# GNN kernel on one core: first row of equal rows from sums of powers of two on TensorE, and the histogram's high-part numbers read from PSUM

## The chip, the cores and the metric

The kernel runs on 1 core of one Trainium2 chip. The metric is the device time of one execution in microseconds (us), and the median over several executions is compared. The engines are named as in the profile: PE is TensorE (PEld its weight loads), DVE is VectorE, ACT is ScalarE, POOL is GpSimd, SP is SyncE; a q behind a name (PEq, DVEq, POOLq) is the engine's instruction queue.

## The reference, cut to what matters

100,000 nodes with 32 features pass through four graph layers that share one list of 50,000 edges sorted by destination; each layer adds its result to x. The change touches two things that the layers need. The first is a table that says, for each node, where its row of edge results lies (`pos_table`), which takes a histogram of the destinations. The second is the neighbour sum of the third layer, in which both ends of an edge give to each other:

```python
rows = jnp.concatenate([i, j]); cols = jnp.concatenate([j, i])
neighbor_sum = jax.ops.segment_sum(conical[cols], rows, num_segments=N_NODES)   # conical: 16 features
deg = jax.ops.segment_sum(jnp.ones_like(rows, dtype=x.dtype), rows, num_segments=N_NODES)
agg = neighbor_sum / jnp.clip(deg, 1.0)[:, None]
```

The part of this sum that goes to the sources of the edges (unsorted) is the scatter with addition that the stage called symmetric below does.

## The kernel before

Edges are padded to 14 chunks (EC) of 28 x 128 (C = 28 edges on each of P = 128 partitions), nodes to 28 chunks (NC) of 28 x 128. The program is a row of stages, each a block in which the engines run lists of their own and meet only at semaphores; at the end of a block all engines wait for each other, so the next stage starts when the last engine is through. In order: `stage_tables`, `stage_attention`, `stage_sage_first`, `stage_sage_second`, `stage_symmetric`, `stage_third_layer`, `stage_relations`. In most of them POOL issues 392 indirect DMAs (one for each of 14 x 28 columns, 128 rows each) one after another.

`stage_tables` (tiles named a_...). POOL makes the constants (L326 to L340), then issues 392 gathers of x by destination into `x_dst` (L342, L343), and last waits for all of them to land. Beside it DVE and PE make the histogram: a destination is cut into a low part (10 bits) and a high part (98 values, HIGH). For each chunk `hot_high` (L350 to L354) compares the high parts of 28 columns with the numbers 0 to 97 in one DVE `tensor_tensor` (is_equal) of 128 x 2744; both its inputs, `part` (float32) and the first 98 columns of `wide` (float16), lie in SBUF, and its result is float16. `hot_low` (L356 to L362) makes four one-hots of 1024 columns of the low parts with `tensor_scalar`, and PE multiplies them (L498) into the count of each of 98 x 1024 nodes. `hot_high` is called 14 times, `hot_low` 98 times. From the counts come the positions (L440 to L451), which are stored; then DVE, ACT and SP normalise the 28 node chunks and store them (L452 to L461, L474 to L479, L313 to L318). `Norm` holds its means in a PSUM bank of 512 columns of which `Norm.USED` = 112 are in use.

`stage_symmetric` (tiles named e_..., L1315 to L1408). Each chunk holds 28 columns of 128 target positions `posF`. Two rows of a column with the same target may not be added by the same indirect DMA, so they are first summed: PE spreads the positions of a column over the partitions (L1392, into PSUM `pB`), DVE compares them with `posF` (L1371, `eq`, 128 x 3584), and PE multiplies `eq` with the 17 values of each row (L1399, into `pS`), which leaves in each row the sum over all equal rows. Only the first of the equal rows may then be written to its target; the others go to a trash row of their own. DVE finds the first by masking `eq` with the triangle `g.before` (L1373, `tensor_tensor`, both inputs in SBUF), summing over the row (L1376, `rank`) and testing for zero (L1378); the index is stored at L1382 as int32. ACT copies the sums to SBUF (L1408), and POOL issues 28 indirect DMAs that add (L1349 to L1357). Index and value buffers are double; DVE and ACT wait, before they write one again, for the adds of two chunks earlier (`wait_added`). The values themselves are made by `sum_back` (L1411 to L1416, two `tensor_tensor`).

Of the kernel before, what the change touches and what calls it, by code (L numbers as in the profile page):

```python
# [4 lines left out]
f32 = mybir.dt.float32  # L5
f16 = mybir.dt.float16
i32 = mybir.dt.int32
ALU = mybir.AluOpType
ACT = mybir.ActivationFunctionType
AX = mybir.AxisListType  # L10

P = 128
F = 32
N, E = 100000, 50000
C = 28
# [14 lines left out]
HIGH = NPAD // LOW  # L30
HID1, HID2 = 64, 128
CON = 16
CW = CON + 1
# [9 lines left out]
def bc_feat(ap, n=F):  # L43
    return ap.unsqueeze(2).to_broadcast([ap.shape[0], ap.shape[1], n])


def bc_tile(ap, n):
    return ap.unsqueeze(1).to_broadcast([ap.shape[0], n, ap.shape[1]])
# [183 lines left out]
def stage_tables(nc, g):  # L232
# [3 lines left out]
    with ExitStack() as ctx, g.sem.stage():  # L236
        sb = lambda name, shape, dt=f32: ctx.enter_context(nc.sbuf_tensor(f"a_{name}", shape, dt))
        S = lambda name: g.sem(f"a_{name}")
# [4 lines left out]
        part = sb("part", [P, 2, ET])  # L243
        wide_i = sb("wide_i", [P, LOW], i32)
        wide = sb("wide", [P, LOW], f16)
        base_i = sb("base_i", [HIGH, LOW], i32)
        base = sb("base", [HIGH, LOW])
        ones = sb("ones", [HIGH, LOW])
        upto, has = sb("upto", [HIGH, LOW]), sb("has", [HIGH, LOW])
        first = sb("first", [HIGH, 1])  # L250
# [22 lines left out]
        flags, all_done, all_kept, deg_rowed, deg_back = S("flags"), S("all_done"), S("all_kept"), S("deg_rowed"), S("deg_back")  # L273
        block = ctx.enter_context(nc.Block())
        w = g.norm

        @block.sync
        def _(sp):
# [70 lines left out]
        def _(dve):  # L349
            def hot_high(c):  # L350
                if c > 1:
                    dve.wait_ge(hots_used, (c - 1) * (C // GROUP))
                nc.vector.tensor_tensor(hoth[:, c % 2], bc_feat(part[:, 1, c * C:(c + 1) * C], HIGH),
                                        bc_tile(wide[:, 0:HIGH], C), ALU.is_equal)  # L354

            def hot_low(n):  # L356
                if n > 1:
# [43 lines left out]
            dve.drain().then_inc(padded, 1)  # L401
            dve.wait_ge(made, 1)
            nc.vector.tensor_copy(wide[:], wide_i[:])
            nc.vector.tensor_copy(base[:], base_i[:])
            nc.vector.tensor_copy(g.relid[:], g.relid_i[:])
            nc.vector.tensor_copy(g.trash[:], g.trash_i[:])
# [120 lines left out]
def part(c):  # L527
    return slice(c * C, (c + 1) * C)
# [785 lines left out]
def stage_symmetric(nc, g):  # L1314

    with ExitStack() as ctx, g.sem.stage():
        sb = lambda name, shape, dt=f32: ctx.enter_context(nc.sbuf_tensor(f"e_{name}", shape, dt))
        S = lambda name: g.sem(f"e_{name}")  # L1320
        SW = lambda name: g.lasting(f"e_{name}")
        eq, eqb = sb("equal", [P, C, P]), sb("equal_before", [P, C, P])
        val, add = sb("values", [P, 2, C, CW]), sb("add_rows", [P, 2, C, CW])
        aidx = sb("add_idx", [P, 2, C], i32)
        rank, shift = sb("rank", [P, C]), sb("shift", [P, C])
        pB = ctx.enter_context(nc.psum_tensor("e_pB", [P, C * P], f32))
        pS = ctx.enter_context(nc.psum_tensor("e_pS", [P, 512], f32))
        val_ready, spread, eq_ready, summed, add_ready, idx_ready = (
            S(x) for x in ("val_ready", "spread", "eq_ready", "summed", "add_ready", "idx_ready"))
        R = len(g.sums)  # L1330
        added = [SW(f"added{b}") for b in range(R)]
        block = ctx.enter_context(nc.Block())

        def wait_added(eng, c):

            for b in range(R):
                eng.wait_ge(added[b], 16 * len(range(b, (c + 1) * C, R)))

        @block.sync
        def _(sp):  # L1340
            g.sem.clear_before(sp)

        @block.gpsimd
        def _(pool):
            for c in range(EC):
                pool.wait_ge(idx_ready, c + 1)
                pool.wait_ge(add_ready, c + 1)
                for t in range(C):
                    b, turn = (c * C + t) % R, (c * C + t) // R  # L1349
                    if turn:  # L1350
                        pool.wait_ge(added[b], 16 * turn)
                    pool.indirect_dma_start(  # L1352
                        out=g.sums[b], out_offset=bass.IndirectOffsetOnAxis(ap=aidx[:, c % 2, t:t + 1], axis=0),
                        in_=add[:, c % 2, t, :], in_offset=None, bounds_check=NTRASH - 1, oob_is_err=True,
                        compute_op=ALU.add).then_inc(added[b], 16)
            wait_added(pool, EC - 1)

        @block.vector
        def _(dve):
            nc.vector.memset(val[:], 1.0)  # L1360
            dve.drain()
            for c in range(EC):
                a = c % 2
                if c > 1:
                    dve.wait_ge(summed, c - 1)
                sum_back(nc, dve, g, g.con_in[:, c, :], g.con[:, c], c, val[:, a, :, 0:CON])
                dve.drain().then_inc(val_ready, 1)
                dve.wait_ge(spread, c + 1)
                if c:
                    dve.wait_ge(summed, c)  # L1370
                nc.vector.tensor_tensor(eq[:], pB[:].rearrange("p (t k) -> p t k", k=P), bc_feat(g.posF[:, part(c)], P), ALU.is_equal)  # L1371
                dve.drain().then_inc(eq_ready, 1)  # L1372
                nc.vector.tensor_tensor(eqb[:], eq[:], bc_tile(g.before[:], C), ALU.mult)  # L1373
                nc.vector.tensor_scalar(shift[:], g.posF[:, part(c)], g.trash[:, 0:1], None, ALU.subtract)
                dve.drain()
                nc.vector.tensor_reduce(rank[:], eqb[:], AX.X, ALU.add)  # L1376
                dve.drain()
                nc.vector.scalar_tensor_tensor(out=shift[:], in0=rank[:], scalar=0.0, in1=shift[:], op0=ALU.is_equal, op1=ALU.mult)  # L1378
                dve.drain()
                if c > 1:  # L1380
                    wait_added(dve, c - 2)
                nc.vector.tensor_scalar(aidx[:, a, :], shift[:], g.trash[:, 0:1], None, ALU.add)  # L1382
                dve.drain().then_inc(idx_ready, 1)

        @block.tensor
        def _(pe):
            for c in range(EC):
                if c:
                    pe.wait_ge(eq_ready, c)
                for t in range(C):  # L1390
                    n = c * C + t
                    last = nc.tensor.transpose(pB[:, t * P:(t + 1) * P], g.posF[:, n:n + 1].to_broadcast([P, P]), g.ident[:])  # L1392
                last.then_inc(spread, 1)
                pe.wait_ge(eq_ready, c + 1)
                pe.wait_ge(val_ready, c + 1)
                if c:
                    pe.wait_ge(add_ready, c)
                for t in range(C):
                    last = nc.tensor.matmul(pS[:, t * CW:(t + 1) * CW], eq[:, t, :], val[:, c % 2, t, :], start=True, stop=True)  # L1399
                last.then_inc(summed, 1)  # L1400

        @block.scalar
        def _(act):
            for c in range(EC):
                act.wait_ge(summed, c + 1)
                if c > 1:
                    wait_added(act, c - 2)
                nc.scalar.copy(add[:, c % 2].rearrange("p t w -> p (t w)"), pS[:, 0:C * CW]).then_inc(add_ready, 1)  # L1408


def sum_back(nc, dve, g, car, fil, c, out):  # L1411

    K = car.shape[1]
    nc.vector.tensor_tensor(out, bc_tile(car, C), bc_feat(g.suf[:, part(c)], K), ALU.mult)
    dve.drain()
    nc.vector.tensor_tensor(out, out, swap(fil), ALU.add)  # L1416
# [483 lines left out]
def build(nc, A, dbg=()):  # L1900
# [15 lines left out]
    with ExitStack() as ctx:  # L1916
# [16 lines left out]
        with ExitStack() as early:  # L1933
            sb1 = lambda name, shape, dt=f32: early.enter_context(nc.sbuf_tensor(name, shape, dt))
            g.w1l, g.w1r, g.w1gr = sb1("w1l", [P, 2, P]), sb1("w1r", [P, 2, P]), sb1("w1gr", [P, P])
            g.b1col, g.b1out = sb1("b1col", [P, 1]), sb1("b1out", [P, F])
            with ExitStack() as attention:
                sb0 = lambda name, shape, dt=f32: attention.enter_context(nc.sbuf_tensor(name, shape, dt))
                g.w0, g.bias0, g.watt = sb0("w0", [P, P]), sb0("bias0", [P, F]), sb0("watt", [P, 3, F])
                g.precut, g.cut0 = sb0("precut", [P, ET]), sb0("cut_inside", [P, ET])  # L1940
                g.srcI, g.dstI = sb0("src", [P, ET], i32), sb0("dst", [P, ET], i32)
                with g.norm.space():
                    stage_tables(nc, g)
                    stage_attention(nc, g)
            with g.norm.space():
                stage_sage_first(nc, g)
# [57 lines left out]
```

## Time and profile before

| | us |
|---|---|
| median of 3 runs | 4964.66 |
| lowest and highest | 4962.52, 4970.22 |
| the profiled execution, own time | 4980.69 |
| its span, first to last instruction | 4979.0 |
| mean granted TensorE clock | 0.67 |

The profiled execution took 16.0 us more than the median (0.3%); its span is 1.7 us less than its own time. In the profile a number after x counts instructions, a time in square brackets is how long the engine stood idle before the instruction, and the name behind the arrow is what ended that. L12 is line 12 of the kernel. "issue" is time in which an engine waited for nothing that the profile shows. Times in the timeline are us from the start of the span; a row there may merge several instructions (its x says how many).

### The profile page before, as it was taken

How to read it: one execution, taken by the hardware profiler on the slowest of the kernel's cores; microseconds unless marked ns; L12 is line 12 of the kernel's file. 1: busy time of each engine (PE TensorE's matmuls, PEld its weight loads, DVE VectorE, ACT ScalarE, POOL GpSimd, SP SyncE). 2: the span in 40 equal slices, each digit the busy share in tenths (PEclk: the TensorE clock that was granted, in tenths of full speed). 3: DMA queues.
4: the chain of work that ended last, by engine and by line, in shares of the span. 5: the costliest groups of instructions: out<-in, count | busy, mean ns of one | idle time of the engine just before them, and what ended most of it. 6: DMA issues, size and time to landing. Idle time of an engine off the chain costs nothing. (4 is left out here: it accounts for less than half of the span.)

```text
span 4979.0 us, 30430 instructions
## 1 busy us (share of the span) xinstructions
PE 2353.3 (47%) x8870; PEld 1415.7 (28%) x8870; DVE 2972.3 (60%) x3595; ACT 933.8 (19%) x1345; POOL 3530.3 (71%) x3150
## 2 busy tenths in 40 slices
PE   7810156665577760000433222167663756656563
PEld 3400033343344440000433222022221433333332
DVE  8865166665677765566532222066664778778784
ACT  0011011211344431111000000044442111111110
POOL 8877676663777717777488888777774577777774
PEclk9955555555799985555555555588886777777776
DMA  1044243432344432222122222345442011110100
GB/s 27 10 123 134 35 89 88 87 84 68 100 143 144 146 125 64 63 77 64 12 5 5 5 5 5 46 141 156 153 148 63 19 31 27 25 31 21 31 25 11
DMA packets 347736, 327.80 MB, mean 66 GB/s; under 512 B 223248, under 2 KB 295835, under 8 KB 346365
## 3 DMA queue, kind: packets, MB, share of 16 engines
q1 hardware_dynamic: 84368, 236.67, 13.3%
q0 software_dynamic: 144256, 45.62, 10.4%
q10 hardware_dynamic: 118944, 43.56, 3.6%
q8 instruction: 70, 1.15, 0.1%
q14 instruction: 98, 0.79, 0.1%
HBM read 170.38 MB, written 156.58 MB: 66 GB/s over the span
## 5 line engine op out<-in xcount | busy, mean ns | idle before, releaser
L1352 POOL DMA_INDIRECT sum_table<-e_add_rows,e_add_idx x392 | 657.1, 1676 | 173.8 <-issue 118.0
L1704 POOL DMA_INDIRECT out_x<-g_out_rows,end_index x392 | 401.2, 1023 | 224.0 <-issue 122.2
L533 POOL DMA_INDIRECT d_ring<-g_table,pos x392 | 392.9, 1002 | 217.9 <-issue 124.2
L533 POOL DMA_INDIRECT c_ring<-x_table,pos x392 | 396.3, 1011 | 204.1 <-issue 121.9
L533 POOL DMA_INDIRECT g_ring<-x_table,pos x392 | 418.8, 1068 | 172.2 <-issue 119.1
L533 POOL DMA_INDIRECT b_ring<-h_table,src x392 | 404.9, 1033 | 180.0 <-issue 116.0
L343 POOL DMA_INDIRECT x_dst<-in_x,dst x392 | 436.2, 1113 | 133.5 <-issue 133.5
L533 POOL DMA_INDIRECT f_ring<-con_table,pos x392 | 419.3, 1070 | 133.7 <-issue 126.8
L1880 PE MATMUL g_pX<-w,g_h_T 128*128 128x512 f32 x784 | 442.7, 716 | 114.9 <-DVEq L1740 114.8
L1617 PE MATMUL f_pH<-f_T,w2in 128*128 128x448 f32 x672 | 316.8, 617 | 277.8 <-DVE f_T L1509 277.8
L1399 PE MATMUL e_pS<-e_values,e_equal 128*128 128x17 f32 x784 | 168.8, 374 | 418.9 <-DVEq L1372 418.9
L164 ACT ACTIVATE norm_sq<-norm_xc 128x896 f32<-128x896 f32 x168 | 158.1, 949 | 856.2 <-DVE norm_xc L137 683.9
L1382 DVE TENSOR_SCALAR e_add_idx<-e_shift,trash 128x28 int32<-128x28 f32 x14 | 3.5, 248 | 478.7 <-DMA sum_table<-e_add_rows,e_add_idx 478.6
L1399 PEld LDWEIGHTS e_pS<-e_values,e_equal 128*128 128x128 f32 x784 | 167.3, 330 | 422.3 <-DVEq L1372 422.3
L1738 DVE TENSOR_TENSOR g_bases<-g_pX,g_rel 128x1024 f32<-128x1024 f32 x196 | 238.7, 1218 | 44.9 <-PE g_pX L1880 37.5
L1617 PEld LDWEIGHTS f_pH<-f_T,w2in 128*128 128x128 f32 x672 | 135.4, 214 | 450.5 <-DVE f_T L1509 288.7
L1579 ACT ACTIVATE f_hid_T<-f_pH,b2col 128x448 f32<-128x448 f32 x336 | 208.1, 635 | 292.2 <-PE f_pH L1617 275.8
L1880 PEld LDWEIGHTS g_pX<-w,g_h_T 128*128 128x128 f32 x784 | 172.9, 233 | 311.6 <-issue 171.5
L1741 DVE TENSOR_REDUCE g_message<-g_bases 128x64 f32<-128x1024 f32 x196 | 239.4, 1221 | 23.7 <-issue 0.9
L144 DVE TENSOR_REDUCE norm_stat<-norm_sq 128x28 f32<-128x896 f32 x168 | 176.6, 1079 | 90.5 <-ACT norm_sq L164 88.1
L498 PE MATMUL a_pcnt<-a_hot_low,a_hot_high 128*98 128x512 f16 x784 | 198.7, 409 | 46.2 <-DVE a_hot_low L361 45.2
L228 PE MATMUL b_pT<-ident,b_h_node 128*128 128x128 f32 x196 | 49.1, 428 | 314.7 <-DMA b_h_node<-h_table 314.7
(342 smaller groups left out, 5250.4 us busy)
## 6 DMA issues: line engine op xcount, KB each, us to landing
f_sums<-sum_table ACTq DMA_DIRECT2D x126, 238.0 KB
sum_table<-c_zero SPq DMA_DIRECT2D x39, 715.0 KB, 5.3
g_table<-c_g SPq DMA_DIRECT2D x42, 448.0 KB, 2.5
g_etype<-in_etype_rows SPq DMA_DIRECT2D x14, 1204.0 KB
h_table<-a_xp SPq DMA_DIRECT2D x28, 560.0 KB, 3.2
a_x<-in_x SPq DMA_DIRECT2D x28, 448.0 KB, 5.0
b_h_node<-h_table ACTq DMA_DIRECT2D x28, 448.0 KB, 4.6
b_x_node<-in_x SPq DMA_DIRECT2D x28, 448.0 KB, 3.5
```

Of the source, the lines that this page charges most:

```text
L144: self.nc.vector.tensor_reduce(self.stat[:, s, 0, :], self.sq[:, s], AX.X, ALU.add).then_inc(self.summed, 1)
L343: pool.indirect_dma_start(out=g.xd[:, t, :], out_offset=None, in_=g.x, in_offset=bass.IndirectOffsetOnAxis(ap=g.dstI[:, t:t + 1], axis=0)) ...
L498: last = nc.tensor.matmul(pcnt[0:HIGH, half * 512:(half + 1) * 512], hoth[:, (t // C) % 2, t % C, :], hotl[:, n % 2, j, half * 512:(half + ...
L533: pool.indirect_dma_start(out=ring[:, t, :], out_offset=None, in_=table, in_offset=bass.IndirectOffsetOnAxis(ap=idx[:, c * C + t:c * C + t ...
L1352: pool.indirect_dma_start(out=g.sums[b], out_offset=bass.IndirectOffsetOnAxis(ap=aidx[:, c % 2, t:t + 1], axis=0), in_=add[:, c % 2, t, :] ...
L1399: last = nc.tensor.matmul(pS[:, t * CW:(t + 1) * CW], eq[:, t, :], val[:, c % 2, t, :], start=True, stop=True)
L1579: nc.scalar.activation(hid[:, n, :], pH[:, n % 4 * 512:n % 4 * 512 + HALF], ACT.Relu, bias=g.b2col[:, 0:1]).then_inc(hid_sb, 1)
L1617: nc.tensor.matmul(pH[:, i * 512:i * 512 + HALF], g.w2in[:, i, :], tsb[:, j % 2, c0:c0 + HALF], start=True, stop=True).then_inc(hid_done, 1)
L1704: pool.indirect_dma_start(out=g.out, out_offset=bass.IndirectOffsetOnAxis(ap=g.endI[:, n:n + 1], axis=0), in_=out[:, c % 2, t, :], in_offs ...
L1738: nc.vector.tensor_tensor(bases[:, d % 2], pX[d % 2][:].rearrange("p (t o b) -> p t o b", t=2, b=NB), rel[:, c % 2, ts, RT - NB:RT].unsque ...
L1741: nc.vector.tensor_reduce(swap(msg[:, :, ts]), bases[:, d % 2], AX.X, ALU.add)
L1880: last = nc.tensor.matmul(pX[d % 2][:, j * 512:(j + 1) * 512], tsb[:, 0, quad], g.w3[:, (2 * d + j) % 4, :], start=True, stop=True)
```

## The change

In `stage_tables` the numbers 0 to 97 are also copied to 98 free columns of the norm's PSUM bank, as float32, and `hot_high` reads them there. In `stage_symmetric` the masked comparison goes. The values get an eighteenth column that holds 2^(63-p) on partition p, made once from an iota; the product on PE gives in that column the sum of the powers of all equal rows, and a row is the first when the sum is at most twice its own power (`first`). The test waits for the product (`summed`), ACT and PE wait for the test (`sums_read`), and `eq` takes the space of the mask as its second buffer.

```diff
 (stage_tables)
+        highs = w.bank[:, Norm.USED:Norm.USED + HIGH]
...
                 nc.vector.tensor_tensor(hoth[:, c % 2], bc_feat(part[:, 1, c * C:(c + 1) * C], HIGH),
-                                        bc_tile(wide[:, 0:HIGH], C), ALU.is_equal)
+                                        bc_tile(highs, C), ALU.is_equal)
...
             nc.vector.tensor_copy(wide[:], wide_i[:])
+            nc.vector.tensor_copy(highs, wide_i[:, 0:HIGH])
 (stage_symmetric)
-        eq, eqb = sb("equal", [P, C, P]), sb("equal_before", [P, C, P])
-        val, add = sb("values", [P, 2, C, CW]), sb("add_rows", [P, 2, C, CW])
+        eq = sb("equal", [P, 2, C, P])
+        val, add = sb("values", [P, 2, C, CW + 1]), sb("add_rows", [P, 2, C, CW])
+        power_i, power, twice = sb("power_i", [P, 1], i32), sb("power", [P, 1]), sb("twice_power", [P, 1])
-        rank, shift = sb("rank", [P, C]), sb("shift", [P, C])
+        first, shift = sb("first", [P, C]), sb("shift", [P, C])
+        sums = pS[:, 0:C * (CW + 1)].rearrange("p (t w) -> p t w", w=CW + 1)
 (POOL)
+            nc.gpsimd.iota(power_i[:], pattern=[[0, 1]], base=(127 + 63) << 23, channel_multiplier=-(1 << 23)).then_inc(powers, 1)
 (DVE, once)
             nc.vector.memset(val[:], 1.0)
+            dve.wait_ge(powers, 1)
+            nc.vector.tensor_copy(power[:], power_i[:].bitcast(f32))
+            dve.drain()
+            nc.vector.tensor_scalar(twice[:], power[:], 2.0, None, ALU.mult)
+            for a in range(2):
+                nc.vector.tensor_copy(val[:, a, :, CW], power[:, 0:1].to_broadcast([P, C]))
 (DVE, for each chunk)
                 dve.wait_ge(spread, c + 1)
-                if c:
-                    dve.wait_ge(summed, c)
-                nc.vector.tensor_tensor(eq[:], pB[:].rearrange("p (t k) -> p t k", k=P), bc_feat(g.posF[:, part(c)], P), ALU.is_equal)
+                nc.vector.tensor_tensor(eq[:, a], pB[:].rearrange("p (t k) -> p t k", k=P), bc_feat(g.posF[:, part(c)], P), ALU.is_equal)
+                nc.vector.tensor_scalar(shift[:], g.posF[:, part(c)], g.trash[:, 0:1], None, ALU.subtract)
                 dve.drain().then_inc(eq_ready, 1)
-                nc.vector.tensor_tensor(eqb[:], eq[:], bc_tile(g.before[:], C), ALU.mult)
-                nc.vector.tensor_scalar(shift[:], g.posF[:, part(c)], g.trash[:, 0:1], None, ALU.subtract)
-                dve.drain()
-                nc.vector.tensor_reduce(rank[:], eqb[:], AX.X, ALU.add)
-                dve.drain()
-                nc.vector.scalar_tensor_tensor(out=shift[:], in0=rank[:], scalar=0.0, in1=shift[:], op0=ALU.is_equal, op1=ALU.mult)
+                dve.wait_ge(summed, c + 1)
+                nc.vector.tensor_scalar(first[:], sums[:, :, CW], twice[:, 0:1], None, ALU.is_le)
+                dve.drain().then_inc(sums_read, 1)
+                nc.vector.tensor_tensor(shift[:], first[:], shift[:], ALU.mult)
                 dve.drain()
                 if c > 1:
                     wait_added(dve, c - 2)
                 nc.vector.tensor_scalar(aidx[:, a, :], shift[:], g.trash[:, 0:1], None, ALU.add)
 (PE)
                     pe.wait_ge(add_ready, c)
+                    pe.wait_ge(sums_read, c)
                 for t in range(C):
-                    last = nc.tensor.matmul(pS[:, t * CW:(t + 1) * CW], eq[:, t, :], val[:, c % 2, t, :], start=True, stop=True)
+                    last = nc.tensor.matmul(sums[:, t, :], eq[:, c % 2, t, :], val[:, c % 2, t, :], start=True, stop=True)
 (ACT)
-                nc.scalar.copy(add[:, c % 2].rearrange("p t w -> p (t w)"), pS[:, 0:C * CW]).then_inc(add_ready, 1)
+                act.wait_ge(sums_read, c + 1)
+                nc.scalar.copy(add[:, c % 2], sums[:, :, 0:CW]).then_inc(add_ready, 1)
```

## Rows read from the trace of the kernel before

**Rows 1.** The page: span, and busy time of each engine.

```profile
span 4979.0 us, 30430 instructions
PE 2353.3 (47%) x8870; PEld 1415.7 (28%) x8870; DVE 2972.3 (60%) x3595; ACT 933.8 (19%) x1345; POOL 3530.3 (71%) x3150
```

**Rows 2.** Busy time by stretch: the histogram, the rest of `stage_tables`, the adding in `stage_symmetric`.

```profile
12.00:265.00 253.00, 206.43 (x866) 105.32 (x866) 222.92 (x434) 3.29 (x2) 204.96 (x149) 0.92 0.08 12
265.00:574.00 309.00, 1.64 (x8) 0.81 (x6) 134.91 (x146) 43.38 (x85) 225.75 (x240) 0.51 0.36 106
2424.00:3201.00 777.00, 222.15 (x1090) 218.90 (x1088) 178.54 (x102) 7.24 (x14) 656.88 (x392) 0.54 0.26 5
```

**Rows 3.** Who waited for whom from 265 to 600 us: total, times, longest.

```profile
DVE b_one_row L706 <- PEq L236: 107.7, 1, 107.7
```

**Rows 4.** Timeline of the histogram around one `hot_high`.

```profile
27.90 1.14 POOL L343 DMA_INDIRECT x_dst<-in_x,dst  x1 [0.31 <-issue]
29.23 3.01 DVE L353 TENSOR_TENSOR a_hot_high<-a_part,a_wide 128x2744 f16<-128x2744 f32 x1
29.35 3.81 POOL L343 DMA_INDIRECT x_dst<-in_x,dst  x1 [0.30 <-issue]
```

**Rows 5.** L343 alone, in 14 windows around its long instructions: their sum.

```profile
sum 51.15, POOL 50.35; mean POOL 3.60
```

**Rows 6.** L343 from 265 to 576 us: ns minimum, median, maximum.

```profile
L343 POOL DMA_INDIRECT x_dst<-in_x,dst x240: 939/945/955, 264.2 to 573.2; - x120
```

**Rows 7.** Timeline of the first chunk of `stage_symmetric`.

```profile
2407.31 3.89 DVE L1371 TENSOR_TENSOR e_equal<-e_pB,pos_f 128x3584 f32<-128x3584 f32 x1 [2.22 <-PE e_pB L1392]
2411.28 12.13 PE L1399 MATMUL e_pS<-e_values,e_equal 128*128 128x17 f32 x56 [4.01 <-DVEq L1372]
2423.45 0.56 ACT L1408 COPY e_add_rows<-e_pS 128x476 f32<-128x476 f32 x1 [31.88 <-PE e_pS L1399]
2424.92 1.62 POOL L1352 DMA_INDIRECT sum_table<-e_add_rows,e_add_idx  x1 [54.59 <-ACT e_add_rows L1408]
```

**Rows 8.** Timeline of a later chunk of `stage_symmetric`, DVE beside POOL.

```profile
2485.49 0.62 DVE L1414 TENSOR_TENSOR e_values<-con_from_after,same_to_end 128x448 f32<-128x448 f32 x1
2485.70 1.84 POOL L1352 DMA_INDIRECT sum_table<-e_add_rows,e_add_idx  x1 [0.30 <-issue]
2487.34 3.89 DVE L1371 TENSOR_TENSOR e_equal<-e_pB,pos_f 128x3584 f32<-128x3584 f32 x1 [0.18 <-issue]
2487.84 1.55 POOL L1352 DMA_INDIRECT sum_table<-e_add_rows,e_add_idx  x1 [0.30 <-issue]
...
2491.35 3.89 DVE L1373 TENSOR_TENSOR e_equal_before<-e_equal,before 128x3584 f32<-128x3584 f32 x1
2491.56 5.11 POOL L1352 DMA_INDIRECT sum_table<-e_add_rows,e_add_idx  x1 [0.30 <-issue]
2495.16 0.23 DVE L1374 TENSOR_SCALAR e_shift<-pos_f,trash 128x28 f32<-128x28 f32 x1
...
2498.84 1.55 POOL L1352 DMA_INDIRECT sum_table<-e_add_rows,e_add_idx  x1 [0.30 <-issue]
2499.44 0.19 DVE L1378 SCALAR_TENSOR_TENSOR e_shift<-e_rank,e_shift 128x28 f32<-128x28 f32 x1
```

**Rows 9.** L1352 alone, in 13 windows around its long instructions: their sum.

```profile
sum 65.48, POOL 64.73; mean POOL 4.98
```

**Rows 10.** L1352: ns minimum, median, maximum.

```profile
L1352 POOL DMA_INDIRECT sum_table<-e_add_rows,e_add_idx x392: 1553/1554/5115, 2424.9 to 3199.6; - x196
```

**Rows 11.** Who waited for whom from 2402 to 3210 us.

```profile
DVE e_add_idx L1382 <- DMA sum_table<-e_add_rows,e_add_idx: 478.6, 12, 41.6
```

**Rows 12.** The page: the chain that ended last, by line.

```profile
DMA g_etype<-in_etype_rows 7%; PE g_pX L1880 3%; DVE g_message L1741 2%; DVE g_bases L1738 2%; DVEq L1740 1%; PE g_pR L1874 1%; DVE norm_xc L137 1%; POOL g_ring L533 1%; DVE g_etype L1730 1%; DVE g_out_rows L847 1%; DVE g_out_rows L1774 1%;
```

**Rows 13.** The page: busy us and mean ns of the matmuls of L1880; their minimum, median, maximum.

```profile
L1880 PE MATMUL g_pX<-w,g_h_T 128*128 128x512 f32 x784 | 442.7, 716 | 114.9 <-DVEq L1740 114.8
...
L1880 PE MATMUL g_pX<-w,g_h_T x784: 592/592/1222, 3861.6 to 4914.0; 128*128 128x512 f32 x196
```

More of the change, by code:

```diff
@@ L1321, in stage_symmetric @@
         SW = lambda name: g.lasting(f"e_{name}")
-        eq, eqb = sb("equal", [P, C, P]), sb("equal_before", [P, C, P])
-        val, add = sb("values", [P, 2, C, CW]), sb("add_rows", [P, 2, C, CW])
+        eq = sb("equal", [P, 2, C, P])
+        val, add = sb("values", [P, 2, C, CW + 1]), sb("add_rows", [P, 2, C, CW])
+        power_i, power, twice = sb("power_i", [P, 1], i32), sb("power", [P, 1]), sb("twice_power", [P, 1])
         aidx = sb("add_idx", [P, 2, C], i32)
-        rank, shift = sb("rank", [P, C]), sb("shift", [P, C])
+        first, shift = sb("first", [P, C]), sb("shift", [P, C])
         pB = ctx.enter_context(nc.psum_tensor("e_pB", [P, C * P], f32))
         pS = ctx.enter_context(nc.psum_tensor("e_pS", [P, 512], f32))
-        val_ready, spread, eq_ready, summed, add_ready, idx_ready = (
-            S(x) for x in ("val_ready", "spread", "eq_ready", "summed", "add_ready", "idx_ready"))
+        sums = pS[:, 0:C * (CW + 1)].rearrange("p (t w) -> p t w", w=CW + 1)
+        powers, val_ready, spread, eq_ready, summed, sums_read, add_ready, idx_ready = (
+            S(x) for x in ("powers", "val_ready", "spread", "eq_ready", "summed", "sums_read", "add_ready", "idx_ready"))
         R = len(g.sums)
```

## The prediction

> **What bounds the kernel now.** I read the page first. POOL is the busiest engine, 3530.3 us of 4979.0, and DVE is busy for 2972.3 [rows 1]; both shares are averages over seven stages, so they say where to look and not what a change is worth. The table of busy time by stretch is next, for the two stages that the diff touches [rows 2]. From 2424 to 3201 us POOL is busy for 656.9 of 777 us; with 0.30 us of issue before each of its 392 adds ("issue" in [rows 8]) it is full: 656.9 + 392 x 0.30 = 774.5. DVE has 178.5 us of work there. It stands still for 478.6 us before it may write the next index, released by the landing of adds [rows 11]. So in `stage_symmetric` only POOL's own pace counts. The same in `stage_tables`: DVE waits 107.7 us at its end for the block to close [rows 3], while POOL's gathers follow one another without a gap until the last starts at 573.2 us [rows 6]. POOL ends this stage too, with over 100 us in hand against DVE. A microsecond off POOL in either stage is a microsecond off the kernel, until 107.7 us are used up in the first one.
>
> What holds POOL up is seen in the timeline. In the histogram a gather takes 3.81 us when it starts beside `hot_high`, against 1.14 us just before [rows 4]. In `stage_symmetric` an add takes 5.11 us beside the mask of L1373, but 1.55 us beside the comparison of L1371 of the same shape and length [rows 8]. The two differ in one thing that fits: L1371 has one input in PSUM and one in SBUF, while L1373 and `hot_high` have both inputs in SBUF. In both cases POOL ends 1.4 or 0.9 us after DVE's instruction (2491.56 + 5.11 against 2491.35 + 3.89; 29.35 + 3.81 against 29.23 + 3.01), so it has waited for the whole of it.
>
> **The change, part by part.**
>
> (1) `hot_high` reads its numbers from PSUM. 14 gathers are long, 50.35 us together [rows 5]. Once L353 has one input in SBUF, as L1371 has, they should be ordinary. Ordinary is 0.945 us beside undisturbing work [rows 6], or, for a gather of the histogram, (204.96 - 50.35) / 135 = 1.145 us [rows 2, 5], since `hot_low` still stretches some. The gain is 50.35 - 14 x 0.945 = 37.1 at most and 50.35 - 14 x 1.145 = 34.3 us at least. I take the middle, 35.7: during `hot_high` POOL will run at 0.945, but the next gather now meets a `hot_low` that the long one hid. DVE's own 3.01 us stay: L1371 gives 3.89 us for 3584 elements with a PSUM input, and L1373 the same without, so the kind of input does not change the length. If it did, nothing would follow: the histogram's end has DVE's 107.7 us of cover. The one new copy of 128 x 98 falls in the stage's start and has the same cover.
>
> (2) The mask goes. 13 of its 14 runs hit an add (the first one comes before POOL starts, see [rows 7]). The 13 long adds are 64.73 us [rows 9]; at 1.554 each [rows 10] they would be 20.20. Gain 44.5 us. The reduction of L1376 goes too (3.9 us x 14 on DVE), and it is worth nothing: DVE stands still for 41.6 us in a chunk [rows 11].
>
> (3) Small instructions on DVE in each chunk: `shift`, the test, the product with `first`, against `shift` and L1378 before. By rows 8 they take 0.2 us each. Before, `shift` ran while POOL was waiting anyway; now it may meet an add. Bounds: an add beside the 0.62 us of `sum_back` with two SBUF inputs takes 1.84 instead of 1.55, so 0.29 us, twice in each of 13 chunks, 7.5 us; the other end is L1378, which has two SBUF inputs and runs at 2499.44 beside an add of 1.55 that shows nothing [rows 8], so 0. I take 1, near L1378, whose size theirs is. Nothing here speaks for a gain.
>
> (4) The start of `stage_symmetric` is the one place where the longer chain is bare, because POOL's first add waits for ACT's copy, which waits for the product [rows 7]. The new DVE work ahead of `sum_back` (three copies and a product of at most 128 x 28, about 0.2 us each, 0.8 together) and POOL's iota lie under the wait of 2.22 us for PE ahead of L1371 [rows 7]. Then `shift` delays `eq_ready` by at most 0.23; the product has 18 columns for 17, nothing or at most 12.13 / 17 = 0.7; the test stands before ACT's copy, 0.2 plus a hand-over of about 0.1. The index comes out beside the copy (0.56). Bounds 0.3 and 1.5; I take 0.7, once.
>
> (5) Steady state. DVE now waits for the product before it makes the index. From the release of one index to the next being ready: the index about 0.3, `sum_back` and a gap until L1371 starts 1.9 us (2487.34 - 2485.49) [rows 8], comparison 3.9, product 12.13, three small ones with drains about 1: 19 us. POOL needs 28 x (1.554 + 0.30) = 51.9 us for a chunk. What was 41.6 us of standing still shrinks by the product's time but gains back the removed 7.8, so some 37 us stay, and PE's transposes (L1392) don't wait for `sums_read`. The second buffer of `eq` is worth nothing: no time was lost at `summed`. Cost 0.
>
> Sum: 35.7 + 44.5 - 1 - 0.7 = 78.5 us. The profiled execution took 4980.7; it would take 4902.2. It was 16.0 us above the median of the runs, 4964.66, and I carry the difference over: 4886.2. Nothing is late next in either stage but POOL's own pace: `stage_tables` still has some 72 us of cover, and later stages start at a barrier each.
>
> What the Trainium skill says of the rows on contention: "SBUF — State Buffer", section "Who interferes with whom", has DVE instructions with two SBUF inputs contend only with a GpSimd instruction's reads, and adds, marked as inferred, that `tensor_tensor` was not seen to stall DMAs since descriptor generation needs the write interface. The trace speaks against that last sentence (3.81 and 5.11 us). By it nothing would be gained; that is rival B. The same section lets a `tensor_scalar` in a two-port mode hold GpSimd off. By that rule `shift` alone would cost POOL up to its own 0.23 us in each of 13 chunks, 3 us where I take 1 for all three, and the sum would be 76.5.
>
> **The rivals.**
> A. `hot_high` still holds POOL up, because something other than the second SBUF input does it (its broadcast over 28 columns, its float16 result). For: no row shows an instruction with a float16 result and a PSUM input. Against: L1371 broadcasts as well and disturbs nothing. Gain 42.8, time 4921.9. Chance 0.08.
> B. The stretching isn't DVE's doing at all; POOL's descriptor work stays as slow. For: the skill's sentence above. Against: 27 long instructions, each ending just after its DVE partner. Time 4964.7 + 0.7 = 4965, within 0.2%. Chance 0.02.
> C. Slower: TensorE's granted clock. In `stage_relations` the matmuls of L1880 take 592 ns at most times and 1222 at others, mean 716 [rows 13]; they hold 3% of the span on the chain [rows 12], 149 us. Should the earlier start find TensorE at the lower of its two levels (1.2 instead of 2.4 GHz) for the whole stage, they would take 149 x 1222 / 716 = 254, 105 us more: 4991. It decides from 78.5 us lost, three quarters of the stage at the low level. Against: the change leaves PE's work there as it is. Chance 0.03.
> D. Slower in another place: POOL waits for each chunk's index, if the chain of (5) were serial with the adds: 13 x 19 = 247 us. It would need a chain of over 51.9 us. Time 5133. Chance 0.01.
>
> **How the numbers follow.** Forecast 0.86, A 0.08, B 0.02, C 0.03, D 0.01. The forecast's bounds: (1) 34.3 to 37.1, (3) 0 to 7.5, (4) 0.3 to 1.5, which gives a gain of 69.8 to 81.3, 4883 to 4895; the runs before spread from 4962.5 to 4970.2, so its own range is 4878 to 4903. For 8 in 10 I reach down to 4874, where a stage's clock happens to help, and up to 4923, to take in A. A measurement of this kernel tells 0.2% (10 us) from no change. Faster by more: 0.94 (forecast and A); within: 0.02; slower by more: 0.04.
>
> **What would show it.** Right: no gather of L343 over 1.5 us beside L353, POOL's busy time in the histogram's 149 or so gathers at about 1.1 us each, the last gather near 537 us instead of 573.2, and DVE's wait at the end of the stage near 72. In `stage_symmetric` no add over 2 us, 392 adds at 1.86 us from start to start, 728 to 735 us for the whole instead of 776. `hot_high` at 3.0 us. Wrong: long gathers at L353 (A), long adds at places where DVE reads PSUM (B), idle time of POOL ahead of adds that ends at the index or at ACT's copy more than once (D), stages after 3208 us of another length than before (C).

## The result, and the profile after

The changed kernel took 4901.3 us (median of 4 runs, 4889.5 to 4909.5), against 4967.4 for the kernel before in the same measurement: ratio 0.9864, interval 0.984 to 0.9889, so 55 to 79 us less. The forecast was 4886.2, with a range of 4874 to 4923. Two more measurements of the same kernel gave 0.9845 (0.9828 to 0.9862) and 0.9852 (0.9835 to 0.9868), 77 and 74 us less. The ratio of mask_half, further below, leaves out one execution that took 5389.9 us at a granted clock of 0.526, where all other executions had 0.67 to 0.68.

The page's head and the stretches that answer to [rows 1, 2]:

```profile
span 4907.7 us, 30413 instructions
PE 2358.0 (48%) x8870; PEld 1420.0 (29%) x8870; DVE 2867.6 (58%) x3586; ACT 933.0 (19%) x1345; POOL 3440.9 (70%) x3151
...
12.00:265.00 253.00, 207.39 (x861) 105.17 (x861) 223.34 (x434) 3.29 (x2) 195.63 (x180) 0.92 0.09 14
265.00:536.00 271.00, 2.43 (x11) 1.31 (x10) 134.90 (x146) 43.38 (x85) 197.12 (x209) 0.51 0.39 119
2387.00:3119.00 732.00, 222.88 (x1085) 219.62 (x1083) 81.68 (x90) 7.21 (x13) 612.50 (x392) 0.54 0.26 5
```

In the histogram POOL (fifth busy time) now gets through 180 gathers in the time of 149, with DVE and PE as busy as before. In the adding DVE's work fell from 178.5 to 81.7 us; that is the mask and the reduction. POOL's own 656.9 fell to 612.5. The experiments below show that the second follows from the place of the mask's input, and not from the amount of DVE's work.

The timeline beside one comparison of high parts, the place of [rows 4], and the row of all gathers, which answers to the one of [rows 6]:

```profile
28.93 1.15 POOL L344 DMA_INDIRECT x_dst<-in_x,dst  x1 [0.30 <-issue]
29.58 3.00 DVE L354 TENSOR_TENSOR a_hot_high<-a_part,norm_bank 128x2744 f16<-128x2744 f32 x1
...
30.38 0.94 POOL L344 DMA_INDIRECT x_dst<-in_x,dst  x1 [0.30 <-issue]
31.63 0.94 POOL L344 DMA_INDIRECT x_dst<-in_x,dst  x1 [0.30 <-issue]
...
L344 POOL DMA_INDIRECT x_dst<-in_x,dst x392: 938/944/1716, 5.4 to 535.1; - x196
```

The comparison is as long as before (3.00 us), and two gathers of 0.94 start under it where one of 3.81 stood. The longest gather of the stage, 1.72 us, stands at 271.6 us, behind the histogram; beside the comparison none is over 1.2. The last gather starts at 535.1 instead of 573.2.

The wait for the end of `stage_tables`, as in [rows 3], and two waits of the symmetric stage, as in [rows 11]:

```profile
DVE b_one_row L708 <- PEq L236: 69.8, 1, 69.8
...
DVE e_add_idx L1392 <- DMA sum_table<-e_add_rows,e_add_idx: 379.8, 12, 33.4
DVE e_first L1386 <- PE e_pS L1410: 170.6, 14, 12.3
```

The cover was said to shrink to 72 us, and it is 69.8. The new wait, DVE for the product, is 12.2 us in each chunk; it comes out of standing still that was there already, and 33 us of that are left. 37 were expected; the prediction left out that a chunk itself gets shorter by the 3.5 us that its long add no longer loses.

The start of `stage_symmetric`, as in [rows 7]:

```profile
2369.08 3.89 DVE L1382 TENSOR_TENSOR e_equal<-e_pB,pos_f 128x3584 f32<-128x3584 f32 x1 [2.90 <-PE e_pB L1402]
2372.89 0.23 DVE L1383 TENSOR_SCALAR e_shift<-pos_f,trash 128x28 f32<-128x28 f32 x1
...
2373.20 12.13 PE L1410 MATMUL e_pS<-e_values,e_equal 128*128 128x18 f32 x56 [4.16 <-DVEq L1384]
...
2385.37 0.25 DVE L1386 TENSOR_SCALAR e_first<-e_pS,e_twice_power 128x28 f32<-128x28 f32 x1 [12.26 <-PE e_pS L1410]
2385.73 0.56 ACT L1420 COPY e_add_rows<-e_pS 128x476 f32<-128x476 f32 x1 [33.55 <-DVEq L1387]
...
2387.20 1.63 POOL L1359 DMA_INDIRECT sum_table<-e_add_rows,e_add_idx  x1 [24.24 <-ACT e_add_rows L1420]
```

The comparison still waits for PE (2.90 us), so the new preparation costs nothing. From its start to POOL's first add it is 18.1 us, against 17.6 in [rows 7]: 0.5 us more. (In other profiles it is 16.4 and 17.6 with the old stage, 17.2 and 18.1 with the new one, as the product takes 11 or 12 us in both.) The product with 18 columns takes 12.13 us as with 17.

A later chunk, as in [rows 8], and the row of all adds, as in [rows 10]:

```profile
2493.39 1.90 POOL L1359 DMA_INDIRECT sum_table<-e_add_rows,e_add_idx  x1 [0.30 <-issue]
2495.04 3.89 DVE L1382 TENSOR_TENSOR e_equal<-e_pB,pos_f 128x3584 f32<-128x3584 f32 x1
...
2497.45 1.55 POOL L1359 DMA_INDIRECT sum_table<-e_add_rows,e_add_idx  x1 [0.30 <-issue]
2498.85 0.23 DVE L1383 TENSOR_SCALAR e_shift<-pos_f,trash 128x28 f32<-128x28 f32 x1
...
2510.46 1.55 POOL L1359 DMA_INDIRECT sum_table<-e_add_rows,e_add_idx  x1 [0.30 <-issue]
...
2511.33 0.25 DVE L1386 TENSOR_SCALAR e_first<-e_pS,e_twice_power 128x28 f32<-128x28 f32 x1 [12.25 <-PE e_pS L1410]
2511.70 0.19 DVE L1388 TENSOR_TENSOR e_shift<-e_first,e_shift 128x28 f32<-128x28 f32 x1
...
L1359 POOL DMA_INDIRECT sum_table<-e_add_rows,e_add_idx x392: 1553/1553/1956, 2387.2 to 3117.4; - x196
```

No add is over 2 us. The small new instructions show on none of the adds beside them. But each of them begins when an add is already under way (2498.85 within the add of 2497.45, 2511.33 and 2511.70 within that of 2510.46), and such adds are not stretched, as mask_sbuf shows below; what they would cost a starting add, no row shows. `sum_back`, which was there before, still stretches one add in most chunks (1.90). The adds go from 2387.2 to 3117.4, 730.2 us, against 774.7.

### The profile page after: what moved, and what is told of

Same layout as the page of the kernel before. It is cut to its first block and busy times, and to the rows that moved or that the text cites. A ratio compares the mean times of both kernels' runs of the same rounds, so it can differ in the third digit from the quotient of the medians.

```text
span 4907.7 us, 30413 instructions
## 1 busy us (share of the span) xinstructions
PE 2358.0 (48%) x8870; PEld 1420.0 (29%) x8870; DVE 2867.6 (58%) x3586; ACT 933.0 (19%) x1345; POOL 3440.9 (70%) x3151
## 5 line engine op out<-in xcount | busy, mean ns | idle before, releaser
L1359 POOL DMA_INDIRECT sum_table<-e_add_rows,e_add_idx x392 | 612.5, 1562 | 143.4 <-issue 118.6
L344 POOL DMA_INDIRECT x_dst<-in_x,dst x392 | 398.2, 1016 | 133.4 <-issue 133.4
L1410 PE MATMUL e_pS<-e_values,e_equal 128*128 128x18 f32 x784 | 168.9, 378 | 376.8 <-DVEq L1384 376.8
L362 DVE TENSOR_SCALAR a_hot_low<-a_wide,a_part 128x1024 f16<-128x1024 f16 x392 | 166.8, 489 | 28.6 <-PE a_pcnt L500 27.3
```

The lines of the kernel that those rows point to most:

```text
L344: pool.indirect_dma_start(out=g.xd[:, t, :], out_offset=None, in_=g.x, in_offset=bass.IndirectOffsetOnAxis(ap=g.dstI[:, t:t + 1], axis=0)) ...
L1359: pool.indirect_dma_start(out=g.sums[b], out_offset=bass.IndirectOffsetOnAxis(ap=aidx[:, c % 2, t:t + 1], axis=0), in_=add[:, c % 2, t, :] ...
L1410: last = nc.tensor.matmul(sums[:, t, :], eq[:, c % 2, t, :], val[:, c % 2, t, :], start=True, stop=True)
```

## The experiments

Stage lengths of the profiles, in us. "Tables" is the start of the last gather into x_dst, "adds" from the first add to the last, "third layer" from its first gather to the first gather of the stage after it.

| kernel | tables | adds | third layer | ratio to before |
|---|---|---|---|---|
| before, first profile | 573.2 | 774.7 | 599.2 | |
| before_again | 565.4 | 772.9 | 597.2 | 0.9999 |
| after, first | 535.1 | 730.2 | 606.8 | 0.9864 |
| after_again | 534.9 | 730.4 | 602.4 | 0.9845 |
| after_third | 535.0 | 730.5 | 599.1 | 0.9852 |
| tables_only | 534.3 | 774.8 | 598.2 | 0.9934 |
| symmetric_only | 569.2 | 731.3 | 604.4 | 0.9909 |
| mask_sbuf | 532.2 | 769.5 | 603.4 | 0.9942 |
| mask_psum | 537.2 | 731.2 | 600.3 | 0.9870 |
| mask_half | 536.4 | 744.2 | 592.9 | 0.9876 |
| highs_in_sbuf | 574.2 | 730.2 | 604.7 | 0.9923 |
| mask_in_place | 535.3 | 731.1 | 600.5 | 0.9858 |
| quick_start | 533.2 | 730.3 | 607.9 | 0.9818 |

### Both kernels again: how much of the 82 us arrives

The first pair of profiles had POOL's first gather of the third layer 82.2 us earlier (3208.1 to 3125.9), but the end only 71.3 us. Expected of before_again:

> The kernel before once more, beside itself. Theory 1 (the two stages gained 82 us, and the stages after them differ from run to run): 1.000, and the third-layer stage, 599 us from its first gather to the next stage's first in the one profile so far, comes out anywhere between 595 and 610. Theory 2 (the changed kernel really slows the later stages): the stage stays at 599, within 2 us.

and of after_again:

> The changed kernel once more. Theory 1: first gather of the third-layer stage 82 us earlier than before, and the end 75 to 82 us earlier, since the 7.6 and 3.3 us that the first profile showed lost later were chance: ratio 0.984 to 0.985. Theory 2: the third-layer stage takes 607 us again, within 2 us, and the ratio is 0.986.

The unchanged kernel gives 0.9999 (0.9989 to 1.001), the changed one 0.9845. The third layer took 597.2 and 602.4 us: the first lies within both theories of before_again, the second within neither stage length of Theory 2, and the ratio and the 78 us between the medians are those of Theory 1. A second thing fell out: the tables stage of the kernel before took 7.8 us less this time. POOL has three pauses in its gathers that the profile books as issue. They stand before the same gathers in all thirteen profiles, each time after 113 more (before gathers 114, 227 and 340), and the second changes its length most, from 3.2 to 7.8 us; first the kernel before in its first profile, then in its second:

```profile
364.18 0.94 POOL L343 DMA_INDIRECT x_dst<-in_x,dst  x1 [7.84 <-issue]
```

```profile
356.43 0.94 POOL L343 DMA_INDIRECT x_dst<-in_x,dst  x1 [3.29 <-issue]
```

So a single pair of profiles overstates or understates a stage by several us. Over all profiles with the comparison of the high parts in SBUF (573.2, 565.4, 569.2, 574.2) the mean is 570.5, over the nine with it in PSUM 534.8: 35.7 us.

### One part alone

tables_only is the kernel before with the copy to `highs` and `hot_high` reading it. symmetric_only is the changed kernel with

```diff
-                                        bc_tile(highs, C), ALU.is_equal)
+                                        bc_tile(wide[:, 0:HIGH], C), ALU.is_equal)
```

and without the copy. Expected:

> The kernel before with only the high-part numbers in PSUM. Theory: no long gather beside the comparison, the last gather 38 us earlier, the adds of the symmetric stage as slow as before (13 over 3.7 us): 38 us less in all, ratio 0.9923. Rival (something else than the operand holds POOL up in this stage, and the gain came with the other part): nothing, 1.000.

> The changed kernel with the comparison of the high parts reading SBUF again. Theory: 14 gathers of 3 to 3.8 us in the histogram, no add over 2 us, the adds 44 us shorter and the start of the symmetric stage 0.5 us longer: ratio 0.9912. With the tables part this adds up to what both give together. Rival (part of the 44 us comes back as a later wait): the third-layer stage longer by several us here too, and not in the kernel with the tables part alone.

tables_only: 0.9934 (0.992 to 0.9947), 33 us by the ratio and 30 by the medians, where 38 were expected; its adds take 774.8 us as before, its tables stage 534.3, which is 31 us less than in before_again beside it and 39 less than in the first profile. symmetric_only: 0.9909 (0.9894 to 0.9924), 45 us; adds 731.3 us, of which the first is stretched by `sum_back` to 2.36 us. 33 and 45 make 78 (each within some 7 us), and both together measured 77 in the same session. Within that noise the parts add up, and each pays in its own stage; rival A of the prediction, that the high parts' comparison would go on holding POOL up, is out. symmetric_only's third layer took 604.4 us, tables_only's 598.2, which speaks a little for the rival of its expectation; see below.

### The mask put back, in three forms

Into the changed kernel, behind the test on the sums:

```diff
                 nc.vector.tensor_scalar(first[:], sums[:, :, CW], twice[:, 0:1], None, ALU.is_le)
+                nc.vector.tensor_tensor(eqb[:, 0:28], eq[:, a, 0:28], bc_tile(g.before[:], 28), ALU.mult)
```

with `bc_tile(pS[:, 0:P], 28)` in mask_psum, and 14 for 28 in mask_half. Expected:

> The changed kernel with the mask's instruction put back between the test and its signal; both inputs in SBUF, 128x3584, the result unused. Theory (the second SBUF input holds POOL up): 13 adds of 5.1 us, 44 us on the adds, and 3.9 us more once before the first add: 48 us over the changed kernel. Rival (the gain came from the test on the sums, or from the shorter chain): nothing but the 3.9.

> The same instruction, 128x3584, one input in SBUF and the other in PSUM (128 columns of the sums), the result unused. Theory: adds at 1.55 beside it, only the 3.9 us before the first add: 4 us over the changed kernel. Rival (a long DVE instruction of any kind holds POOL up): as the kernel with both inputs in SBUF, 48 us.

> Both inputs in SBUF, half the length (128x1792, some 2.0 us). Theory (POOL waits for the whole instruction, wherever its add had got to): 13 adds of about 1.55 + 3.5 - 1.95 = 3.1 us, 20 us on the adds and 2 us at the start: 22 us over the changed kernel. Rival (a fixed price per collision): 44 and 2.

The timeline of one chunk, mask_sbuf:

```profile
2570.54 1.55 POOL L1360 DMA_INDIRECT sum_table<-e_add_rows,e_add_idx  x1 [0.30 <-issue]
2571.57 3.88 DVE L1388 TENSOR_TENSOR e_equal_before<-e_equal,before 128x3584 f32<-128x3584 f32 x1
2572.39 4.49 POOL L1360 DMA_INDIRECT sum_table<-e_add_rows,e_add_idx  x1 [0.30 <-issue]
```

mask_psum:

```profile
2568.37 3.88 DVE L1388 TENSOR_TENSOR e_equal_before<-e_equal,e_pS 128x3584 f32<-128x3584 f32 x1
2569.20 1.55 POOL L1360 DMA_INDIRECT sum_table<-e_add_rows,e_add_idx  x1 [0.30 <-issue]
```

mask_half:

```profile
2567.16 1.55 POOL L1360 DMA_INDIRECT sum_table<-e_add_rows,e_add_idx  x1 [0.30 <-issue]
2568.18 2.02 DVE L1388 TENSOR_TENSOR e_equal_before<-e_equal,before 128x1792 f32<-128x1792 f32 x1
2569.01 2.61 POOL L1360 DMA_INDIRECT sum_table<-e_add_rows,e_add_idx  x1 [0.30 <-issue]
```

The same instruction of the same length, 0.8 us ahead of an add: with the second input in SBUF the add takes 4.49 us, with it in PSUM 1.55. The adds take 769.5 and 731.2 us, and by the medians (4938.8 and 4902.4) there are 36 us between the two kernels. That is the mechanism, taken by itself. It also shows the price more closely than I had put it. The add that is under way when DVE begins is not stretched (2570.54 + 1.55 runs past 2571.57). The next one is stretched by what is left of DVE's instruction when it starts: 2571.57 + 3.88 - 2572.39 = 3.06 us left, 2.94 longer; in mask_half 1.19 left and 1.06 longer. I had expected 20 us of mask_half, from the 3.5 us of the old kernel less the shorter length; 14 came (744.2 - 730.3), since 0.8 us pass here before the next add starts and in the old kernel 0.2 did (2491.35 and 2491.56 in [rows 8]). A fixed price per collision is out too. mask_sbuf missed its 44 us (it has 39.3, 769.5 less 730.2) for the same reason. The two adds over 2 us of mask_psum (2.35 at its start, and 2.04) begin beside `sum_back`, which has both inputs in SBUF.

### Place or type of the operand

highs_in_sbuf is the changed kernel with

```diff
-        highs = w.bank[:, Norm.USED:Norm.USED + HIGH]
+        highs_sb = sb("highs", [P, HIGH])
+        highs = highs_sb[:]
```

> The changed kernel with the high-part numbers as float32 in an SBUF tile of their own. Theory (the place of the operand decides): 14 gathers of 3 to 3.8 us, 38 us over the changed kernel, as with the float16 numbers. Rival (the float16 type of the second input holds POOL up): no long gather, 0.

```profile
30.25 3.00 DVE L355 TENSOR_TENSOR a_hot_high<-a_part,a_highs 128x2744 f16<-128x2744 f32 x1
30.75 3.42 POOL L345 DMA_INDIRECT x_dst<-in_x,dst  x1 [0.30 <-issue]
...
56.90 4.21 POOL L345 DMA_INDIRECT x_dst<-in_x,dst  x1 [0.30 <-issue]
57.18 3.01 DVE L355 TENSOR_TENSOR a_hot_high<-a_part,a_highs 128x2744 f16<-128x2744 f32 x1
```

The last gather starts at 574.2 us, and the ratio is 0.9923 (0.9901 to 0.9945), about the loss of the whole tables part against the changed kernel's 0.9845 to 0.9864 in other sessions. Beside each of the 14 comparisons one gather takes 3.1 to 4.2 us. float32 in SBUF holds POOL up just as float16 did; the change to float32 did nothing.

The second pair of rows is an exception to what mask_sbuf showed: the gather had begun 0.28 us before DVE's instruction and was held up all the same, until 0.92 us after its end. A second one does so at 230.17 us (4.20). Adds that had begun as little as 0.13 us before the mask were not held up (before_again, 2421.70 against 2421.83, 1.55 us). In both exceptions a `hot_low` was still running when the gather began; whether that is the reason, no run shows.

### The old test with its mask reading PSUM

mask_in_place has the tables part, the old test and no powers. DVE compares a second time in place, and the mask reads that; PE spreads the next chunk only after the mask:

```diff
                 dve.drain().then_inc(eq_ready, 1)
-                nc.vector.tensor_tensor(eqb[:], eq[:], bc_tile(g.before[:], C), ALU.mult)
+                equal = pB[:].rearrange("p (t k) -> p t k", k=P)
+                nc.vector.tensor_tensor(equal, equal, bc_feat(g.posF[:, part(c)], P), ALU.is_equal)
+                dve.drain()
+                nc.vector.tensor_tensor(eqb[:], equal, bc_tile(g.before[:], C), ALU.mult)
```

> The kernel before with the tables part, and the old test by the mask and the rank; but DVE compares once more in place, in PSUM, and the mask reads that copy, so it has one input in SBUF. No powers of two, no eighteenth column. Theory (only the operand's place counts; DVE has room for 3.9 us more in each chunk): adds at 1.55 throughout, 730 us for the adds, the first add at most 1 us later than before: as the changed kernel, ratio 0.984 to 0.985. Rival (the shorter work on DVE matters): DVE comes late and the adds take longer, 0.990 or more.

```profile
2501.47 3.90 DVE L1377 TENSOR_TENSOR e_pB<-e_pB,pos_f 128x3584 f32<-128x3584 f32 x1
...
2503.53 1.55 POOL L1355 DMA_INDIRECT sum_table<-e_add_rows,e_add_idx  x1 [0.30 <-issue]
2505.39 1.55 POOL L1355 DMA_INDIRECT sum_table<-e_add_rows,e_add_idx  x1 [0.30 <-issue]
2505.45 3.89 DVE L1379 TENSOR_TENSOR e_equal_before<-e_pB,before 128x3584 f32<-128x3584 f32 x1
2507.25 1.55 POOL L1355 DMA_INDIRECT sum_table<-e_add_rows,e_add_idx  x1 [0.30 <-issue]
```

0.9858 (0.9843 to 0.9873), beside 0.9852 for the changed kernel in the same session: no difference that the intervals show. The adds take 731.1 us; only the first, beside `sum_back`, is over 2 us (2.43). That is so with about 12 us more of DVE work in every chunk than the changed kernel has (4 us more than the old one). The sums of powers are one way to get rid of an instruction with two SBUF inputs; they are not what gains.

### A version that beats both

quick_start lets POOL begin when 8 of the first chunk's 28 columns are through. For chunk 0 every engine works in two parts with semaphores of their own; on PE:

```diff
+                    for h in range(H):                       # cols = slice(0, 8), slice(8, 28)
+                        pe.wait_ge(eq0, h + 1)
+                        if h:
+                            pe.wait_ge(rd0, h)
+                            pe.wait_ge(ad0, h)
+                        for t in range(C)[cols[h]]:
+                            last = nc.tensor.matmul(sums[:, t, :], eq[:, 0, t, :], val[:, 0, t, :], start=True, stop=True)
+                        last.then_inc(sm0, 1)
```

> The changed kernel with its first chunk of the symmetric stage in two parts of 8 and 20 columns, so that POOL's first adds wait for 8 columns only. Theory (the start is bare, everything in it counts): first add some 12 us earlier against the start of the stage, the second part ready before the eighth add is through, 12 us less in all than the changed kernel, ratio 0.982. Rival (the later stages take it back, as they may have done with 5 to 10 us of the change's): ratio as the changed kernel's, and the third-layer stage longer.

> The changed kernel a third time, beside the two above. If the first result's 66 us was chance and the two stages' 82 us mostly arrive: ratio 0.984 to 0.985 as in the second measurement. The third-layer stage, 606.8 and 602.4 us so far against 597.2 to 599.2 with the old symmetric stage: by chance it falls anywhere between 593 and 607, by an effect of the change it is again over 600.

```profile
2362.75 1.23 DVE L1392 TENSOR_TENSOR e_equal<-e_pB,pos_f 128x1024 f32<-128x1024 f32 x1
...
2369.07 0.27 ACT L1465 COPY e_add_rows<-e_pS 128x136 f32<-128x136 f32 x1 [20.45 <-DVEq L1400]
...
2370.70 1.63 POOL L1366 DMA_INDIRECT sum_table<-e_add_rows,e_add_idx  x1 [11.29 <-DVEq L1404]
...
2378.57 0.44 ACT L1465 COPY e_add_rows<-e_pS 128x340 f32<-128x340 f32 x1 [9.23 <-DVEq L1400]
```

POOL stands idle for 11.29 us before its first add instead of 24.24 (after_again has 24.16 and after_third 21.90, since PE spread the first chunk's positions in 6.1 us and multiplied in 12.1 in the one, 4.8 and 11.2 in the other; so it is 11 to 13 us less), and the second part's copy is done at 2379.0, when POOL is at its fifth add. The ratio is 0.9818 (0.9802 to 0.9834), 17 us under after_third (0.9852) in the same session, where 12 were expected; by the medians, 4882.8 and 4892.1, it is 9. The two intervals only just part, and after_again's overlaps with that of quick_start, so the gain is surer from the stage than from the whole. The third layer took 607.9 us, as the rival had it, but the gain was not taken back. By median and ratio it is the fastest kernel of the study.

## Why the prediction held

(1) **hot_high.** Forecast 35.7 us, bounds 34.3 and 37.1. The first pair of profiles shows 38.1, the means of all profiles 35.7. That the middle of the bounds came out to the tenth is luck. The busy time of the 392 gathers, which has none of the pauses in it, is 436.1 us in the mean of the four profiles with the numbers in SBUF and 398.9 in the nine with them in PSUM, 37.1 us less, which is the upper bound: the gathers under `hot_high` run at 0.94 us, and I had taken up to 0.2 us off each for nothing. The pauses, by chance, are 1.4 us longer in the nine. DVE's instruction kept its length, as taken from the pair L1371 and L1373.

(2) and (3) **The mask and the small instructions.** Forecast 44.5 less 1. The adds took 774.7, 772.9 and 774.8 us with the old test, 730.2 to 730.5 in the three profiles of the changed kernel, 43.8 less in the mean. The small instructions cost nothing that a row shows. The row that I took for the lower bound of 0 was misread, though: L1378 at 2499.44 begins 0.6 us into the add of 2498.84 [rows 8], and an add under way is not stretched, whatever the size of DVE's instruction. The same holds for the new instructions here, so this term came to nothing by the phase between the engines, which is luck and not its size. Also misread was the wait "for the whole of it": a DMA waits for what is left of DVE's instruction when it starts, 3.68 us of 3.89 in [rows 8]. The reduction's 54 us of DVE were worth nothing, as said: mask_in_place keeps them and is no slower.

(4) **The start.** Forecast 0.7, measured 0.5 in the first pair of profiles.

(5) **Steady state.** The new wait is 12.2 us, 33 us of standing still are left beside it, and the cost is 0.

The sum by stages is 35.7 to 38 + 43.8 - 0.5, or 79 to 81 us, against a forecast of 78.5. The three measurements gave 66, 77 and 74. So the steps of the sum were right in size. The median of the first measurement lay 15 us above the forecast. 2.8 us of that are the base: I started from 4964.66, and in the measurement itself the kernel before had 4967.44. For the rest there are two candidates, for which the sum has no term, and no run parts them. One is spread: four runs of the changed kernel lay 20 us apart. The other may be the third layer: 597.2 to 599.2 us in the three profiles with the old symmetric stage as it was, 592.9 to 607.9, mean 602.2, in the ten with a new one. It would be some 4 us given back. The profiles show where such a difference lies: POOL's gathers of the stage take 543 to 547 us in all thirteen, while from its last gather to the first of the next stage it is 53 to 55 us in the three and 49 to 62 in the ten. But after_third has 599.1 and mask_half 592.9, and nothing in that stage was changed, so it stays open whether it is an effect of the change; three profiles on one side don't settle it. My range had no term for such a loss except through rival C.

Of the rivals, A is refuted by tables_only, C did not come (the granted clock was 0.67 before and 0.67 to 0.68 after, and the matmuls of L1880 took 716 ns in the mean before and 707 to 715 in three profiles after), D did not come (POOL waited for ACT's copy once, at the start). B rested on a sentence of the Trainium skill, "SBUF — State Buffer", section "Who interferes with whom": that a `tensor_tensor` was not seen to stall DMAs, since it takes only the pair's read side. mask_sbuf and mask_psum measure the opposite for these indirect DMAs, 4.49 against 1.55 us, so the measurement decides. The section's main rule, that a DVE instruction with two SBUF inputs contends with a GpSimd instruction that reads SBUF, agrees with mask_sbuf, mask_psum, mask_in_place and highs_in_sbuf; that the issue of an indirect DMA is an instruction that reads SBUF, no run shows by itself.

## What to carry to other kernels

Where POOL issues indirect DMAs back to back and sets the end of a stage, look in the timeline for long ones among them and read what DVE was doing: here a long two-input instruction with both inputs in SBUF cost the next DMA what was left of it, even though DVE was mostly idle in the adding. Putting one input in PSUM took the price away without making the instruction shorter; the reduction, which has one input in SBUF, cost nothing.

One input in SBUF is no safe sign, however. After the change the 180 gathers of the histogram still take 195.6 us, 26 more than at 0.944 each, and the timeline shows where most of it is: a gather beside `hot_low` takes 1.14 us in the mean (119 gathers of the first profile after, 23 us over 0.944 in all), one beside `hot_high` alone 0.94 (23 gathers). `hot_low` is a `tensor_scalar` of 128 x 1024 in float16 with one tensor as input and one number for each partition. What in it costs the gathers time was not tested, and these 23 us are the largest such loss left in the two stages; on the adds only 3.5 us over 392 x 1.554 are left.

In a stage like this the first DMA's preparation is bare as well. Splitting it gained 11 to 13 us in its stage, more than the 3.5 us that anything further taken off DVE could gain on the adds.

## What the runs showed that I had not expected

POOL's run of gathers has pauses of 3 to 8 us at the same three places in every profile, with nothing in the profile to release them; one of them was 7.84 us in one profile of the kernel before and 3.29 in the next. An add that is already being issued when DVE's instruction starts is not stretched at all, in any of the profiles read for it (before, before_again, tables_only, mask_sbuf, mask_half), so the price of a collision hangs on the phase between the two engines: 3.56 us for 3.89 us of DVE in the old kernel, 2.94 for the same instruction in mask_sbuf. With gathers it is not as clear: two of highs_in_sbuf, begun 0.28 us before DVE's instruction, waited for the whole of it.
